# Context projections of a decoder layer's fold as three products of split operands, split by GpSimd

## The chip, the cores and the metric

The kernel runs on 1 core of a Trainium2 chip. The metric is the device time of one execution in microseconds (us). The five engines of the core are named as in the profile: PE (TensorE matmul) and PEld (its weight loads), DVE (VectorE), ACT (ScalarE), POOL (GpSimd) and SP (SyncE, which here only issues DMAs).

## The reference, cut to what matters

One decoder layer on `x` of 4 batches x 1024 rows x 256: a gated recurrence, then a cross attention over 64 context rows per batch plus one "null" row, then a feed-forward layer with weights quantised to three values and activations to 8 bits. The change concerns how keys and values of the cross attention are made, and what follows at once:

```python
q = split_heads(einsum('bnd,df->bnf', x, Wq)) * 64 ** -0.5         # 16 heads of 64
kv = einsum('bmc,cf->bmf', context, Wkv)                           # context 4 x 64 x 512, Wkv 512 x 2048
k, v = split_heads(kv[..., :1024]), split_heads(kv[..., 1024:])    # a null key and a null value are put before them
attn = softmax(einsum('bhid,bhjd->bhij', q, k))
out = merge_heads(einsum('bhij,bhjd->bhid', attn, v))
out = einsum('bnf,fd->bnd', out, Wout)
x = x + layernorm(out) * ln_scale + ln_bias
x = x + bitlinear(silu(gate(z)) * up(z), w_down)                   # z = layernorm(x), the feed-forward layer
```

## The kernel before, in words

Each engine has its instruction stream written out by hand, in the order in which it is executed; semaphores tie the streams together. There is no scheduler: an engine that waits holds back all that is written behind the wait.

**Stage 1** (`stage1`, `groups`) runs over 8 groups of 4 tiles of 128 rows: normalise, transpose, project with fp32r products of split operands (a high and a low part, three products: hi x hi, lo x hi, hi x lo), sigmoid, scan on DVE, residual. At its end lie the ternary quantisation of the feed-forward weights (`rounded` on POOL, L520 and L523; `ternary` on DVE, L903) and, for the last groups, the statistics of the second layernorm (`stats2` on DVE up to L914; POOL raises them to a power, L533).

**The fold** comes between stage 1 and the loop over tiles. Since the context is small, keys are multiplied into Wq and values into Wout once, so that a tile needs only scores = x * M and out = p * VW. The program numbers 16 projections `kv_T(i)`: 0 to 7 for keys (one pair of heads each), 8 to 15 for values. A projection (L1362 to L1370) is four fp32 products of 128x128 weights with 128x256 of the transposed context `ctxT`; it appears in rows as L1279 with operands `region_b,VW` (keys) or `region_b` alone (values), as 8 records. Then:

- ACT copies it to `kvT` (`put_kvT`, L734), with the null row subtracted.
- `fold_keys(i)` (PE, L1383) multiplies it with Wq's transpose; ACT takes the high part `Mhi` out of PSUM (L742), DVE the low part `Mlo` (L1032). The PE stream runs `kv_T(i + 2)`, `fold_keys(i)` for i = 0 to 7; before the last of them come the transposes of tiles 0 and 1 (`pair_T(0, 0)`, L1419), whose copies are `xT2hi` (ACT, L771) and `xT2lo` (DVE, L1048).
- Then PE runs tile 0's scores (twelve 128x512 fp32r products, L1279 with `Mhi`, `Mlo`, `xT2hi`, `xT2lo`), `kv_T(10)`, `fold_values(0)` (L1400), `kv_T(11)`, `kv_T(12)`, `fold_values(1)`, tile 1's scores, `kv_T(13)`, `kv_T(14)`, `fold_values(2)`, `pair_T(1, 1)`, the null values (L1410), `kv_T(15)`, `fold_values(3)`. The results are copied to `VW` by DVE (`put_values_first`, L1042) and ACT (`put_values_second`, L752).
- Softmax of tiles 0 and 1 runs beside it: maximum and subtraction on DVE (L1065, L1069, L1070), exponential on ACT (L826), sum and reciprocal on DVE (L1076, L1081), multiplication with the reciprocal on POOL (`probabilities`, L577). POOL also sums Wout's blocks for the null value (`wsum`, L554, L557).

**The loop over tiles** (`stages2_3`, n = 0 to 31, then a tail) runs scores of tile n+2, transposes of the probabilities of tile n (L1530, L1538), out of tile n (L1550, L1553, L1558), and the feed-forward layer of earlier tiles (gate, up, down). ACT alternates between the tables of Exp and Silu: it loads Silu at L786, in `silu_gate` (L783 to L792), and Exp at L826. In a step ACT runs `norm_out` (L779), the two copies of `pT` (L857, L860), `silu_gate`, `quantise_h` (L803), `norm3` (L810), `norm2` (L756), `exponential`. On POOL a step has `add_output` (L562 to L566), `probabilities`, `cast_h` (L590), `deviation3` (L609 to L613), `deviation4`, `quantise_z`.

## Time and profile before

| | |
|---|---|
| median of 3 runs | 496.48 us (495.41 to 497.45) |
| the profiled execution | 498.77 us |
| its span, first to last instruction | 497.0 us |
| busy in the span | PE 462.5 us (93%), PEld 362.3 (73%), DVE 401.7 (81%), ACT 329.1 (66%), POOL 308.9 (62%) |
| mean granted TensorE clock | 0.987 of full speed |
| chain of waits, by engine | PE 80%, DVE 6%, POOL 3%, DMA 3%, the rest 2% or less each |

Busy shares are sums over the whole span. The chain of waits is followed back from the last instruction, at each step to what released it; an edit gains time only where it shortens this chain, and no further than to the next chain beside it. In the rows a time is in us from the start of the span unless it is marked ns. A row of a timeline can hold several instructions of one kind ("x8"); neighbours on PE overlap in their records, as a product's end is modelled. Stage 1 ends at about 98.8 us, the fold lasts from there to 158.6 us, the tail begins at about 465 us.

### The profile page before, as it was taken

The page shows a single profiled execution, that of the slowest core. Times are in us where ns is not written, and L with a number is a line of the kernel's source. Part 1 is how long each engine was busy: PE and PEld are TensorE (multiplying, and loading weights), DVE is VectorE, ACT ScalarE, POOL GpSimd, SP SyncE. Part 2 cuts the span into 40 slices and gives each one's busy share as a digit, 9 for nine tenths or more (in the row PEclk, how much of TensorE's full clock was granted, in tenths as well). Part 3 has the DMA queues.
Part 4 walks back from the last instruction along what each step waited for, and adds up shares of the span by engine and source line. Part 5 has one row for each costly group of instructions (what it writes and reads, how often), then busy time and mean ns, then how long its engine had stood idle before and what let it go on. Part 6 is the DMA issues. An engine that isn't in the chain of part 4 may idle for free.

```text
span 497.0 us, 7915 instructions
## 1 busy us (share of the span) xinstructions
PE 462.5 (93%) x2504; PEld 362.3 (73%) x2532; DVE 401.7 (81%) x882; ACT 329.1 (66%) x429; POOL 308.9 (62%) x465
## 2 busy tenths in 40 slices
PE   1989999999799999999999999999999999999664
PEld 0768888777577888787878777778778787876332
DVE  4789988974455688999989989899898998995883
ACT  4556543245335354898888888889788888886560
POOL 2234555650011468788788788787877878878850
PEclk9999999999899999999999999999999999999996
DMA  8997000240000000012232121212222222222352
GB/s 263 325 365 272 3 0 1 42 86 0 1 1 1 1 0 7 7 32 45 51 44 49 38 58 39 54 38 47 50 44 48 52 45 44 49 43 53 65 120 65
DMA packets 67129, 31.72 MB, mean 64 GB/s; under 512 B 49680, under 2 KB 65296, under 8 KB 67088
## 3 DMA queue, kind: packets, MB, share of 16 engines
q1 hardware_dynamic: 67088, 31.21, 25.0%
q8 instruction: 21, 0.34, 0.3%
q14 instruction: 20, 0.16, 0.1%
HBM read 15.21 MB, written 4.19 MB: 39 GB/s over the span
## 4 chain that ended last, share of the span: by engine, by line
PE 80%; DVE 6%; POOL 3%; DMA 3%; SPq 2%; issue 2%; ACT 2%; another core or an unknown queue 0%; DVEq 0%; ACTq 0%; POOLq 0%
PE psum L1279 37%; PE psum L1553 10%; PE psum L1558 10%; PE psum L1295 10%; DMA xs<-in_x_dram 3%; PE psum L1530 3%; PE psum L1538 2%; SPq L409 2%; PE psum L1383 2%; PE psum L1419 2%; PE psum L1400 2%; PE psum L1314 1%; PE psum L1330 1%; DVE amax L1112 1%; PE psum L1550 1%
## 5 line engine op out<-in xcount | busy, mean ns | idle before, releaser
L577 POOL TENSOR_TENSOR region_d<-region_d,rden 128x1024 f32<-128x1024 f32 x30 | 57.1, 1905 | 13.4 <-DVE rden L1081 13.1
L1553 PE MATMUL psum<-VW,region_d 128*128 128x256 f32 x256 | 60.6, 380 | 0.2
L1558 PE MATMUL psum<-VW,region_d 128*128 128x256 f32 x256 | 60.5, 379 | 0.0
L1279 PE MATMUL psum<-Mhi,xT2hi 128*128 128x512 f32 x128 | 54.2, 424 | 3.3 <-DVE xT2lo L1048 3.3
L1065 DVE TENSOR_REDUCE mx<-psum 128x8 f32<-128x512 f32 x64 | 44.0, 687 | 15.5 <-PE psum L1279 14.5
L1105 DVE SCALAR_TENSOR_TENSOR region_c<-psum,hzw,region_c 128x1024 f32<-128x1024 f32 x32 | 41.1, 1283 | 17.0 <-ACT region_c L791 16.8
L1558 PEld LDWEIGHTS psum<-VW,region_d 128*128 128x128 f32 x256 | 48.6, 190 | 6.6
L1553 PEld LDWEIGHTS psum<-VW,region_d 128*128 128x128 f32 x256 | 46.3, 190 | 6.5 <-ACT region_d L857 0.6
L1279 PE MATMUL psum<-Mhi,xT2lo 128*128 128x512 f32 x128 | 50.9, 397 | 0.0
L1279 PE MATMUL psum<-Mlo,xT2hi 128*128 128x512 f32 x128 | 50.4, 394 | 0.0
L1070 DVE SCALAR_TENSOR_TENSOR region_d<-mx,psum 128x512 f32<-128x512 f32 x60 | 40.9, 681 | 1.0
L529 POOL TENSOR_TENSOR pw_out<-pw_in,expo 128x8 f32<-128x8 f32 x8 | 13.2, 1648 | 43.1 <-DVE pw_in L943 43.1
L1112 DVE TENSOR_REDUCE amax<-region_c 128x1 f32<-128x1024 f32 x32 | 39.0, 1218 | 0.9
L1279 PE MATMUL psum<-wgT,region_d 128*128 128x512 bf16 x123 | 32.3, 379 | 5.7 <-DMA region_d<-region_c 5.5
L791 ACT ACTIVATE region_c<-psum,hzw 128x1024 f32<-128x1024 f32 x32 | 35.7, 1114 | 2.4 <-remote 1.7
L803 ACT ACTIVATE region_c<-region_c,qr 128x1024 int16<-128x1024 f32 x31 | 35.3, 1139 | 2.3 <-DVE qr L1163 1.9
L1076 DVE TENSOR_REDUCE den<-region_d 128x16 f32<-128x1040 f32 x30 | 36.7, 1223 | 0.0
L826 ACT ACTIVATE region_d<-region_d 128x1040 f32<-128x1040 f32 x30 | 32.2, 1072 | 5.6 <-DVE region_d L1070 5.3
L590 POOL CAST region_d<-region_c 128x1024 bf16<-128x1024 int16 x31 | 32.2, 1038 | 4.5 <-ACT region_c L803 4.5
L1295 PE MATMUL psum<-xT1hi,w1hi 128*128 128x512 f32 x96 | 32.1, 416 | 2.2 <-ACT xT1hi L693 1.2
L786 ACT ACT_TABLE_LOAD x26 | 33.4, 1283 | 0.5
L857 ACT ACTIVATE region_d<-psum 128x512 f32<-128x512 f32 x32 | 19.1, 596 | 21.4 <-PE psum L1530 21.3
(159 smaller groups left out, 1163.5 us busy)
## 6 DMA issues: line engine op xcount, KB each, us to landing
out_dram<-xs SPq DMA_DIRECT2D x32, 128.0 KB, 1.9
xs<-in_x_dram SPq DMA_DIRECT2D x1, 2560.0 KB, 13.7
VW<-in_L_xattn_Wkv_dram SPq DMA_DIRECT2D x1, 2048.0 KB, 12.3
region_b<-in_L_xattn_Wkv_dram SPq DMA_DIRECT2D x1, 2048.0 KB, 16.5
xs<-in_x_dram SPq DMA_DIRECT2D x3, 512.0 KB, 6.5
region_w<-in_L_ffn_w_gate_dram SPq DMA_DIRECT2D x2, 512.0 KB, 9.6
region_w<-in_L_ffn_w_up_dram SPq DMA_DIRECT2D x2, 512.0 KB, 8.0
region_w<-in_L_ffn_w_down_dram SPq DMA_DIRECT2D x8, 128.0 KB, 5.7
```

What stands on the lines that cost most here:

```text
L577: pool.tensor_tensor(p_of(t).rearrange("p (h j) -> p h j", j=MK), e[:, :, 0:MK], rden[:, v, :].unsqueeze(2).broadcast_to([P, H, MK]), ALU. ...
L791: act.activation(hid3[v], banks(gate_bank(n), 2).rearrange("p b n -> p (b n)"), ACT.Silu, scale=hzw[:, (n - 5) % 4, 2:3]).then_inc(silu_re ...
L803: act.activation(nq3, hid3[t % 2], ACT.Copy, scale=qr[:, t % 2, 0:1]).then_inc(hq_done, 1)
L1065: dve.tensor_reduce(mx[:, hh, :], scores, AX.X, ALU.max).then_inc(max_done, 1)
L1070: dve.scalar_tensor_tensor(out=e[:, :, 0:MK], in0=mx[:, hh, :].unsqueeze(2).broadcast_to([P, HB, MK]), scalar=0.0, in1=scores, op0=ALU.max ...
L1076: dve.tensor_reduce(den[:, :], e_of(n).rearrange("p (h j) -> p h j", j=J), AX.X, ALU.add) \
L1105: dve.scalar_tensor_tensor(out=hid3[v], in0=banks(2, 2).rearrange("p b n -> p (b n)"), scalar=hzw[:, (n - 5) % 4, 3:4], in1=hid3[v], op0=A ...
L1112: dve.tensor_reduce(amax[:, v, 0:1], hid3[v], AX.X, ALU.max, apply_absolute_value=True) \
L1279: mm = pe.matmul(dst, lhsT, rhs, start=i == 0, stop=i == len(terms) - 1)
L1295: mm = pe.matmul(bank(b), lhsT, rhs, start=i == 0, stop=i == len(terms) - 1)
L1553: pe.matmul(bank(7, D), pT[:, pair, :], VW[:, batch(n), pair, :], start=False, stop=False)
L1558: mm = pe.matmul(bank(7, D), pT[:, pair, :], VW[:, batch(n), pair, :], start=False, stop=pair == HC - 1)
```

## The change

1. **Projections.** `kv_T(i)` becomes twelve fp32r products of 128x256 in place of four fp32 ones: high weights x high context, high weights x low context, low weights x high context (four column blocks each). The last four wait for the low weights alone (`kvw_ready`), the first eight for the high ones (`kvw_hi`).
2. **Splitting.** The context's high part is ACT's copy as before, now as fp32r; its low part is a new 128x1024 subtraction on DVE, put before `ternary(1)`. The weights are split by POOL, 128x512 per projection: a cast to fp32r, then a subtraction (`split_kvw(i)`). There are two buffers, so split i waits for projection i - 2. Splits 0 to 3 lie at the end of POOL's stage 1, 4 to 9 between the additions of `wsum`, 10 to 13 after them, 14 and 15 between `probabilities(0)` and `probabilities(1)`.
3. **Order around tile 0.** `kv_T(10)` goes ahead of tile 0's scores on PE. ACT's `xT2_pair(0, 0)` and DVE's `xT2_lesser(0, 0)` go ahead of the last pair's copies of `M`.
4. **Room.** The split parts use the memory of stage 1's `xT1hi` and `xT1lo`. The exponentials of tiles 0 and 1 lie in the late pairs of `VW` in place of `region_c`, so both `put_values(2)` now wait for `probabilities(1)` (`p_ready` 2). `probabilities` of tiles 0 and 1 is two 128x512 products each. `p` and `pT` lie elsewhere in `region_d`.
5. **ACT's waits.** The wait for the transposed feed-forward weights moves from before `put_kvT(0)` to `put_keys_hi(0)`.
6. **Last steps.** In step 30 ACT loads Silu's table at the start of the step, in place of after the copies of `pT`; in step 31 `silu_gate` comes first on ACT.

```diff
+        ctxThi = xT1hi_flat[:, 0:CC * BM].rearrange("p (k n) -> p k n", k=CC)
+        kvwhi = xT1hi_flat[:, CC * BM:].rearrange("p (r k n) -> p r k n", r=2, k=CC)
+        kvwlo = xT1lo_flat[:, 0:CC * BM].rearrange("p (r k n) -> p r k n", r=2, k=CC)
+        ctxTlo = xT1lo_flat[:, CC * BM:].rearrange("p (k n) -> p k n", k=CC)
...
+        late_pairs = VW[:, :, HC // 2:, :].rearrange("p b c n -> p b (c n)")
+        wsum = VW[:, B - 1, HC - 1, :]
...
+            def split_kvw(i):
+
+                w = (wk if i < HC else wv)[:, :, (i % HC) * P:(i % HC + 1) * P]
+                pool.wait_ge(wk_loaded if i < HC else wv_loaded, 16)
+                if i == 0:
+                    pool.wait_ge(q_psum, NG)
+                if i > 1:
+                    pool.wait_ge(fT_psum, i - 1)
+                pool.tensor_copy(kvwhi[:, i % 2, :, :], w).then_inc(kvw_hi, 1)
+                pool.wait_ge(kvw_hi, i + 1)
+                pool.tensor_tensor(kvwlo[:, i % 2, :, :], w, kvwhi[:, i % 2, :, :].bitcast(F32), ALU.subtract) \
+                    .then_inc(kvw_ready, 1)
...
             groups(stage1)
+            split_kvw(3)
...
             for pair in range(2, HC):
+                split_kvw(pair + 2)
                 pool.wait_ge(wout_summed, pair - 1)
                 pool.tensor_tensor(wsum, wsum, wout[:, pair, :], ALU.add).then_inc(wout_summed, 1)
+            for i in range(HC + 2, HC + 6):
+                split_kvw(i)
...
             probabilities(0)
+            split_kvw(2 * HC - 2)
+            split_kvw(2 * HC - 1)
+            probabilities(1)
...
+                if q == 2:
+                    act.wait_ge(p_ready, 2)
                 act.wait_ge(fold_psum, HC + q + 1)
...
                 if isinstance(g, int) and g == NG - 1:
+                    dve.wait_ge(ctxT_ready, 1)
+                    dve.tensor_tensor(ctxTlo.rearrange("p k n -> p (k n)"), banks(0, 2).rearrange("p b n -> p (b n)"),
+                                      ctxThi.rearrange("p k n -> p (k n)").bitcast(F32), ALU.subtract) \
+                        .then_inc(ctxT_lo_ready, 1)
                     ternary(1)
...
-                w, pair = (wk if i < HC else wv), i % HC
-                group(bank(i % 2, BM), [(w[:, k, pair * P:(pair + 1) * P], ctxT[:, k, :]) for k in range(CC)]) \
-                    .then_inc(fT_psum, 1)
+                pe.wait_ge(kvw_hi, i + 1)
+                for j, (w, c_) in enumerate(((kvwhi, ctxThi), (kvwhi, ctxTlo), (kvwlo, ctxThi))):
+                    if j == 2:
+                        pe.wait_ge(kvw_ready, i + 1)
+                    for k in range(CC):
+                        mm = pe.matmul(bank(i % 2, BM), w[:, i % 2, k, :], c_[:, k, :], start=j == 0 and k == 0,
+                                       stop=j == 2 and k == CC - 1)
+                mm.then_inc(fT_psum, 1)
...
+            kv_T(HC + 2)
             pe.wait_ge(m_lo, 2 * HC)
             for hh in range(2):
                 scores_half(0, hh, 0, 0, 0)
-            kv_T(HC + 2)
             fold_values(0)
```

Where the instructions stand. PE, from the last key fold to the first value fold, before (L1279 with `region_b` is a projection, L1383 the key fold, L1400 the value fold; the rows left out are the rest of tile 0's twelve products):

```order
L1419 MATMUL psum<-ident,region_d 128x128 x4
L1279 MATMUL psum<-region_b 128x256 x4
L1383 MATMUL psum<-region_b,VW 128x256 x4
L1279 MATMUL psum<-Mhi,xT2hi 128x512
L1279 MATMUL psum<-Mlo,xT2hi 128x512
L1279 MATMUL psum<-Mhi,xT2lo 128x512
...
L1279 MATMUL psum<-region_b 128x256 x4
L1400 MATMUL psum<-region_b 64x256 x16
```

The same place now (L1433 is a projection, L1448 the key fold, L1465 the value fold):

```order
L1484 MATMUL psum<-ident,region_d 128x128 x4
L1433 MATMUL psum<-xT1hi 128x256 x4
L1433 MATMUL psum<-xT1lo,xT1hi 128x256 x4
L1433 MATMUL psum<-xT1hi,xT1lo 128x256 x4
L1448 MATMUL psum<-region_b,VW 128x256 x4
L1433 MATMUL psum<-xT1hi 128x256 x4
L1433 MATMUL psum<-xT1lo,xT1hi 128x256 x4
L1433 MATMUL psum<-xT1hi,xT1lo 128x256 x4
L1340 MATMUL psum<-Mhi,xT2hi 128x512
L1340 MATMUL psum<-Mlo,xT2hi 128x512
...
L1465 MATMUL psum<-region_b 64x256 x16
```

A projection has three rows of four products, and projection 10 stands before the scores instead of behind them.

POOL, from its last rounding to tile 0's probabilities, before:

```order
L523 TENSOR_SCALAR region_w<-region_w 128x2048
L533 TENSOR_TENSOR rstd<-ve,expo 128x4 x2
L551 COPY nvsel<-nulls 128x1 x2
L554 TENSOR_TENSOR region_c<-region_b 128x256
L557 TENSOR_TENSOR region_c<-region_c,region_b 128x256 x6
L577 TENSOR_TENSOR region_c<-region_c,rden 128x1024
```

And now, as far as split 4 and the first addition behind it (L543 and L545 are the cast and the subtraction of a split, L556 the power, L585 the addition to `wsum`):

```order
L543 CAST xT1hi<-VW 128x512
L545 TENSOR_TENSOR xT1lo<-VW,xT1hi 128x512
L556 TENSOR_TENSOR rstd<-ve,expo 128x4
L543 CAST xT1hi<-VW 128x512
L545 TENSOR_TENSOR xT1lo<-VW,xT1hi 128x512
L556 TENSOR_TENSOR rstd<-ve,expo 128x4
L543 CAST xT1hi<-VW 128x512
L545 TENSOR_TENSOR xT1lo<-VW,xT1hi 128x512
L579 COPY nvsel<-nulls 128x1 x2
L581 TENSOR_TENSOR VW<-region_b 128x256
L543 CAST xT1hi<-VW 128x512
L545 TENSOR_TENSOR xT1lo<-VW,xT1hi 128x512
```

Splits 2 and 3 stand behind the two powers, which wait for DVE's statistics, and each later addition has a split before it.

DVE, at the end of the last group's work, now (L1053 is the product that was L1003, L1057 the context's low part, L953 `ternary`, L959 to L964 `stats2`):

```order
L1053 TENSOR_TENSOR region_a<-psum,region_a 128x1024
L1057 TENSOR_TENSOR xT1lo<-psum,xT1hi 128x1024
L953 TENSOR_SCALAR region_w<-region_w 128x2048
L969 SCALAR_TENSOR_TENSOR nmr<-mv,rstd 128x4
L959 BN_STATS st<-xs 128x6 x4
```

Before, the row of L1057 was not there and `ternary(1)` followed the product at once.

## Rows read from the trace of the kernel before

**Rows 1.** The page, busy time, share of the span and instructions of each engine
```profile
PE 462.5 (93%) x2504; PEld 362.3 (73%) x2532; DVE 401.7 (81%) x882; ACT 329.1 (66%) x429; POOL 308.9 (62%) x465
```

**Rows 2.** Chain of waits in the fold: start us, length us, what
```profile
127.44 1.09 PE psum L1383 x8
...
128.55 0.61 ACT Mhi L742
...
129.18 1.29 DVE Mlo L1032 x2
130.47 0.61 DVE xT2lo L1048
...
143.08 1.89 PE psum L1400 x32
...
156.62 1.96 PE psum L1400 x32
...
161.07 1.38 PE psum L1279 x6
162.45 0.12 PE psum L1550
```

**Rows 3.** Timeline of PE, projection 10 behind tile 0's scores
```profile
135.24 2.31 PE L1279 MATMUL psum<-region_b 128*128 128x256 f32 x8
```

**Rows 4.** Busy by stretch, tile 0's scores and after: length, engines, granted clock
```profile
131.20:139.40 8.20, 8.19 (x53) 5.97 (x53) 4.07 (x6) 1.43 (x2) 0.00 (x0) 0.79 0.00 0
```

**Rows 5.** Groups of instructions of POOL: busy us, mean ns, idle before
```profile
L577 POOL TENSOR_TENSOR region_d<-region_d,rden 128x1024 f32<-128x1024 f32 x30 | 57.1, 1905 | 13.4 <-DVE rden L1081 13.1
...
L590 POOL CAST region_d<-region_c 128x1024 bf16<-128x1024 int16 x31 | 32.2, 1038 | 4.5 <-ACT region_c L803 4.5
...
L620 POOL TENSOR_SCALAR region_d<-region_d,qr 128x256 f32<-128x256 f32 x32 | 15.4, 482 | 0.6 <-DVE qr L1147 0.6
...
L538 POOL TENSOR_TENSOR xs<-xs,region_b 128x1024 f32<-128x1024 f32 x5 | 12.0, 2396 | 0.0
...
L557 POOL TENSOR_TENSOR region_c<-region_c,region_b 128x256 f32<-128x256 f32 x6 | 4.4, 726 | 0.5
```

**Rows 6.** Timeline of POOL at the end of stage 1
```profile
92.37 3.03 POOL L520 TENSOR_SCALAR region_w<-region_w,wrecip 128x2048 f32<-128x2048 f32 x1
...
106.14 1.01 POOL L533 TENSOR_TENSOR rstd<-ve,expo 128x4 f32<-128x4 f32 x1 [4.24 <-DVE ve L914]
```

**Rows 7.** Timeline of DVE, end of stage 1 and softmax of tiles 0, 1
```profile
85.97 1.20 DVE L926 TENSOR_TENSOR xT1lo<-psum,xT1hi 128x1024 fp32r<-128x1024 f32 x1
...
92.32 1.22 DVE L903 TENSOR_SCALAR region_w<-region_w 128x2048 bf16<-128x2048 f32 x1
...
97.72 1.22 DVE L903 TENSOR_SCALAR region_w<-region_w 128x2048 bf16<-128x2048 f32 x1
...
105.89 0.17 DVE L914 TENSOR_SCALAR ve<-mv 128x4 f32<-128x4 f32 x1
...
139.60 1.25 DVE L1042 COPY VW<-psum 128x512 f32<-128x512 f32 x2
...
151.91 0.25 DVE L1081 RECIPROCAL rden<-den 128x16 f32<-128x16 f32 x1
```

**Rows 8.** Timeline of ACT, context copy and end of the fold
```profile
97.45 1.03 ACT L707 ACTIVATE region_b<-psum 128x1024 f32<-128x1024 f32 x1 [3.99 <-PE psum L1343]
...
153.33 1.08 ACT L752 ACTIVATE VW<-psum 128x512 f32<-128x512 f32 x2 [1.44 <-PE psum L1400]
154.30 0.60 ACT L771 ACTIVATE xT2hi<-psum 128x512 fp32r<-128x512 f32 x1
156.04 0.47 ACT L734 ACTIVATE region_b<-psum,nulls_neg 128x256 f32<-128x256 f32 x1 [1.14 <-PE psum L1279]
```

**Rows 9.** Last steps: table load on ACT (timeline), busy by stretch (PE, PEld, DVE, ACT, POOL)
```profile
449.79 1.28 ACT L786 ACT_TABLE_LOAD   x1
446.80:465.20 18.40, 16.44 (x88) 11.70 (x87) 12.64 (x35) 11.89 (x16) 16.00 (x30) 1.00 0.25 54
```

More of the change, by code:

```diff
@@ L168, in decoder_layer @@
         f = carve(region_b, [("wq", KD * INNER), ("wout", HC * D), ("ctx", 2 * CTX),
-                             ("wv", CC * INNER), ("ctxT", CC * BM),
+                             ("wv", CC * INNER), ("gap", CC * BM),
                              ("kvT", 4 * BM)])
@@ L257, in decoder_layer @@
         ctxT_ready = sem("ctxT_ready")
+        ctxT_lo_ready = sem("ctxT_lo_ready")
+        kvw_hi = sem("kvw_hi")
+        kvw_ready = sem("kvw_ready")
         wqT_psum = sem("wqT_psum")
@@ L546, in stage1 @@
                     rounded(2)
+                    split_kvw(0)
+                    split_kvw(1)
+                if isinstance(g, int) and g == NG:
+                    split_kvw(2)
             groups(stage1)
+            split_kvw(3)
             pool.wait_ge(nvsel_zero, 1)
@@ L629, in stages2_3 @@
                     add_output(n - 1)
-                if exists(n + 1, T):
+                if n > 0 and exists(n + 1, T):
                     probabilities(n + 1)
@@ L737, in put_keys_hi @@
             def put_keys_hi(i):
+                if i == 0:
+                    act.wait_ge(wT_ready[0], 16)
+                    act.wait_ge(wT_ready[1], 16)
                 act.wait_ge(fold_psum, i + 1)
@@ L816, in _ @@
                 put_kvT(i + 1)
+                if i == HC - 1:
+                    xT2_pair(0, 0)
                 put_keys_hi(i)
@@ L825, in exponential @@
                 act.wait_ge(sim_sub, 2 * t + 2)
-                act.activation(e_of(t), e_of(t), ACT.Exp, scale=-1.0).then_inc(exp_done, 1)
-            xT2_pair(0, 0)
+                e = e_of(t) if t < 2 else e2[:, t % 2, :]
+                act.activation(e, e, ACT.Exp, scale=-1.0).then_inc(exp_done, 1)
             put_kvT(HC + 1)
+            put_kvT(HC + 2)
             exponential(0)
-            put_kvT(HC + 2)
             put_kvT(HC + 3)
@@ L849, in stages2_3 @@
                 even = u4 % 2 == 0 and exists(n, T - 4)
+                if n == T - 2:
+                    act.preload_act_table(ACT.Silu)
+                if n == T - 1:
+                    silu_gate(n, v)
                 if exists(n - 1, T):
@@ L861, in stages2_3 @@
                         .then_inc(pT1_ready, 1)
-                if exists(n - 5, T):
+                if exists(n - 5, T) and n < T - 1:
                     silu_gate(n, v)
@@ L1067, in softmax_half @@
                 if hh == 1:
-                    null = e_of(n).rearrange("p (r h j) -> p r h j", r=2, j=J)[:, :, :, MK]
+                    null = e_of(n).rearrange("p r (h j) -> p r h j", j=J)[:, :, :, MK]
                     dve.tensor_scalar(null, mx[:, :, :], 0.0, None, ALU.max).then_inc(shift_done, 1)
```

62 lines of the change are left out of this document (37 added, 25 removed).

## The prediction

> **What bounds the kernel now.** I read the page first: PE is busy for 93% of the span [rows 1], and the chain of waits lies on PE for 80% of it. So an edit must shorten PE's own work or its waits. I then followed the chain through the fold, then the timelines of all engines there. Three things stand in them.
>
> In the key phase PE never waits: the last key fold ends at 127.44 + 1.09 = 128.53 [rows 2]. The way to tile 0's scores is then serial: ACT's copy, DVE's low part, and DVE's low part of the tile, 0.61 + 1.29 + 0.61 us [rows 2], and PE is idle for 2.7 us until 131.2. Behind that wait the granted clock is 0.79 on average over 131.2 to 139.4 [rows 4], a mixture of both levels: tile 0's scores last from 131.2 to 135.24 [rows 3], 4.0 us, whereas six such products at 2.4 GHz take 1.38 us [rows 2], so twelve take 2.76. After the fold's end at 156.62 + 1.96 = 158.58 [rows 2] the loop over tiles is bound by PE, and what the fold gains or loses should pass to the end unchanged.
>
> **The price of a new projection on PE.** The projection of four fp32 products in the slow stretch shows 2.31 us [rows 3]. For a 128x256 product of fp32r the only row is L1550: the next product starts 0.12 us after it [rows 2], about half of the 0.23 us of 128x512. Twelve in a row make 12 x 0.12 = 1.44 us. The other bound is the 128x512 price, 12 x 0.23 = 2.76. I take 0.12, as it is the same shape and type.
>
> **The price of a split on POOL.** No row has a cast of 512 elements to fp32r. L620 does 256 elements in 0.482 us and L590 1024 in 1.038 [rows 5]; between them 512 take 0.67. The subtraction: L557 (256) takes 0.726 and L538 (1024) 2.396 [rows 5], so 512 take 1.28; L577 does 1024 in 1.905, where one operand is 16 values repeated. I take 1.28, since the subtraction, like L538 and L557, reads two full tensors; with L577's rate it would be 0.95. With a hop after each cast a split is S = 2.0 us. Bounds: 0.52 + 0.95 + a hop, 1.55; and the whole 1024-element rows, 1.04 + 1.91 + a hop, 3.0. A split and the addition behind it (0.73 [rows 5] and a hop, 0.8) make 2.8 us per pair. PE needs 1.44 + 1.09 = 2.5 per pair. **POOL becomes the bound of the key phase.**
>
> **When POOL starts.** The context copy ends at 97.45 + 1.03 = 98.48 [rows 8]. DVE waits for it, subtracts for 1.20 (L926 [rows 7] has the same shape) and starts `ternary(1)` at 99.65 instead of 97.72 [rows 7]. All behind it slips by 1.9 us, so the last group's statistics come at 108.0 instead of 106.06 [rows 7], and POOL's power, which waited for them at 106.14 [rows 6], ends at 109.05. Split 3 is queued behind it. From there: split 3 (2.0), the two copies and the first sum (1.05, of it 0.73 as L557), six splits with five additions between them (12.0 + 4.0): split 9 is done at 128.1. Its last four products (0.48) and the last key fold (1.09) follow: **the key phase ends at F = 129.7, 1.2 us later than before.** All PE work before F, split 0 to 2 included, is earlier than its split.
>
> **From F on.** Now `xT2lo` is made before, so scores start at F + 2.0 (0.61 + 1.29 and hops [rows 2]) = 131.7. Projection 10 fits in that gap (its split ends at 130.95), so PE isn't idle and I expect the clock to stay at 2.4 GHz: 2.76 for the scores. The PE work between the scores and the last value fold is now shorter than the softmax beside it, so new waits set the pace:
> - From a tile's scores to its reciprocal takes, for tile 1, from 143.08 + 1.89 = 144.97 [rows 2] to 151.91 + 0.25 = 152.16 [rows 7], 7.2 us. For tile 0: 138.9.
> - `put_values_first(0)` is queued behind it, 1.25 [rows 7]: 140.1. `fold_values(1)` waits for this (PE alone would be there at 139.3), ends at 142.05 with 1.9 [rows 2].
> - Tile 1's scores start there; its reciprocal is at 149.25.
> - `probabilities(1)`, 1.905 in one piece [rows 5], 2.1 in two: 151.35. Split 15 is done at about 148, before it.
> - ACT is held by the new wait for this: `put_values_second(2)` 1.1, `xT2_pair` 0.5, `put_kvT(15)` 0.5 [rows 8]: 153.55.
> - `fold_values(3)` takes 1.96 [rows 2]: **155.5 instead of 158.58, 3.1 us earlier.**
> From F to this end are 25.8 us, where they were 30.05: a gain of 4.25 after F, of which 1.2 are lost before it.
>
> **The last steps.** In step 30 the table load (at 449.79, 1.28 us [rows 9]) moves ahead of the copies, so silu comes some 0.7 us earlier and the copies of `pT` 0.5 later. But from 446.8 to 465.2 POOL runs 30 instructions, busy for 16.0 of 18.4 us with a hop of under 0.1 us behind each [rows 9], and waits for neither. I take 0 to 0.1 us. Two halves instead of one whole of `probabilities(0)` and the moved buffers cost nothing on the path: PE waits elsewhere.
>
> The sum against the profiled execution: 497.0 - 3.1 of span. That execution took 498.77 us with what lies around it; the median of the runs is 496.48, 2.3 lower. I take the gain off the median: **493.4 us**.
>
> **A rule that speaks against the change.** POOL's L520, 2048 elements, took 3.03 us beside DVE's L903 [rows 6, 7], where twice L590's 1.04 [rows 5] would be 2.1. Splits 1 and 2 lie beside `ternary(1)` and `ternary(2)` and may take 1 us more each; both are done before what follows waits for them (the powers wait for DVE until 102.8 and 108.0), so F doesn't move. The Trainium skill (GPSIMD Engine Reference, Key points) says that GpSimd shares its SBUF interfaces with VectorE and contends with instructions in a 2-port mode or with two SBUF inputs. By that rule the key phase is free of it, since DVE's low parts of M read one operand from PSUM. The pair of rows on L520 agrees with the first half; no row shows the second.
>
> **Rivals.**
> 1. *GpSimd is quicker than taken.* With S = 1.55 F is 7 x 0.45 = 3.2 earlier: 126.5, and the time 490.2. For it: L577's rate. Against: L538 and L557 agree on a slower one. Chance 0.2 for clearly quicker (S below 1.8).
> 2. *GpSimd is slower, and the key phase eats the gain.* It decides from S = 2.0 + 3.1 / 7 = 2.44 us on: F is then 132.8. A cast to fp32r from rows with a stride, or a DVE that shares the memory through the whole phase, could do it; with another 1 us per split, as L520 had [rows 6], S = 3.0, F = 136.7, and the time is 500.4. Against: L557 ran in this very phase beside the same DVE work at 0.726. Chance 0.14 (of it 0.09 slower than before by over 0.5%).
> 3. *fp32r at 256 columns isn't faster in a row than at 512.* Then a projection is 2.76 us on PE and a key pair 3.85; seven of them and a tile pair's transposes behind the first key fold, at 110.9 with three such projections ahead of it, make F about 138, and PE's own work after it (six projections 16.6, two scores 5.5, four folds 7.6, transposes and null 1.0) ends at about 169: 507 us. For it: L1550 stands alone between other shapes, no row has two in a row. Against: 0.12 us sufficed there with a new weight load. Chance 0.05.
> 4. *The gain is partly cancelled*: PE now waits about 1 us before key pair 1, at `fold_values(1)` and at `fold_values(3)`; should the clock fall behind one, the scores' loss of 1.3 us comes back, or the softmax chain is longer than tile 1's was: 495 to 496. Chance 0.13.
>
> **How the numbers follow.** The forecast has 0.48, with 492 to 494.6 as its own range (S from 1.8 to 2.15). 0.5%, 2.5 us, is about what a measurement of this kernel can tell from no change; the forecast lies 0.6 beyond it, so I give faster all of rival 1 and three quarters of the forecast: 0.2 + 0.36 = 0.56. Same: the rest of the forecast 0.12, rival 4, and 0.05 of rival 2: 0.30. Slower: 0.14. The range leaves out the quick end of rival 1, the slow half of rival 2 and rival 3: 490.5 to 498.
>
> **What would show it right or wrong.** Right: in the key phase the new products wait for POOL's subtraction, about 2.8 us per pair, and split 9 is done at about 128; scores of tile 0 take 2.8 us with the clock at 1.00; `fold_values(3)` waits for ACT. The POOL rows of the cast (0.67) and the subtraction (1.28) are the first to read. Wrong: PE without waits in the key phase (rival 1), products 0.23 us apart (rival 3), subtractions of 1.7 us or more (rival 2), or a loop over tiles that doesn't keep its distance from the fold.

## The result, and the profile after

| | before | after |
|---|---|---|
| median | 496.7 us (13 runs, 495.41 to 499.77) | 498.19 us (13 runs, 497.68 to 501.05) |
| ratio, 95% interval | | 1.0034 [1.0017, 1.0050] |
| profiled execution, span, mean granted clock | 498.77 us, 497.0 us, 0.987 | 498.17 us, 496.3 us, 0.992 |

The forecast was 493.4 us and a range of 490.5 to 498.0. The change made the kernel slower by 0.34%, within what I had called "same" and 0.2 us outside the range. Measured once more on another chip (a0_again below) it took 497.12 us, ratio 1.0021: inside the range, but again no gain. The page of after, its part on busy time:

```profile
PE 458.8 (92%) x2568; PEld 363.3 (73%) x2596; DVE 406.2 (82%) x883; ACT 328.7 (66%) x429; POOL 340.6 (69%) x499
```

PE is busy for 3.7 us less than in [rows 1], POOL for 31.7 us more, and the median did not fall. The fold tells why. First POOL at the end of stage 1, where [rows 6] had the last power at 106.14 (timeline: start us, length us, instruction, in brackets the idle time before it and what ended it):

```profile
97.80 1.28 POOL L545 TENSOR_TENSOR xT1lo<-VW,xT1hi 128x512 fp32r<-128x512 f32 x1
99.02 0.61 POOL L543 CAST xT1hi<-VW 128x512 fp32r<-128x512 f32 x1
99.71 2.14 POOL L545 TENSOR_TENSOR xT1lo<-VW,xT1hi 128x512 fp32r<-128x512 f32 x1
103.75 1.01 POOL L556 TENSOR_TENSOR rstd<-ve,expo 128x4 f32<-128x4 f32 x1 [1.90 <-DVE ve L964]
104.72 1.68 POOL L543 CAST xT1hi<-VW 128x512 fp32r<-128x512 f32 x1
106.48 1.29 POOL L545 TENSOR_TENSOR xT1lo<-VW,xT1hi 128x512 fp32r<-128x512 f32 x1
109.67 1.01 POOL L556 TENSOR_TENSOR rstd<-ve,expo 128x4 f32<-128x4 f32 x1 [1.90 <-DVE ve L964]
...
111.32 1.29 POOL L545 TENSOR_TENSOR xT1lo<-VW,xT1hi 128x512 fp32r<-128x512 f32 x1
...
125.85 0.74 POOL L585 TENSOR_TENSOR VW<-VW,region_b 128x256 f32<-128x256 f32 x1
126.52 0.62 POOL L543 CAST xT1hi<-region_b 128x512 fp32r<-128x512 f32 x1
127.22 1.29 POOL L545 TENSOR_TENSOR xT1lo<-region_b,xT1hi 128x512 fp32r<-128x512 f32 x1
128.47 0.73 POOL L585 TENSOR_TENSOR VW<-VW,region_b 128x256 f32<-128x256 f32 x1
```

A split undisturbed is 0.61 + 1.28 with a hop, 1.93 us; a split and its addition come every 128.47 - 125.85 = 2.62 us. Splits 2 and 3 stand behind the powers and wait for DVE. DVE at the same place (compare [rows 7]):

```profile
98.27 1.22 DVE L1057 TENSOR_TENSOR xT1lo<-psum,xT1hi 128x1024 fp32r<-128x1024 f32 x1 [0.71 <-ACT xT1hi L749]
99.41 1.30 DVE L953 TENSOR_SCALAR region_w<-region_w 128x2048 bf16<-128x2048 f32 x1
100.64 1.24 DVE L969 SCALAR_TENSOR_TENSOR nmr<-mv,rstd 128x4 f32<-128x4 f32 x1
...
104.72 1.22 DVE L953 TENSOR_SCALAR VW<-region_w 128x2048 bf16<-128x2048 f32 x1
...
106.98 0.80 DVE L969 SCALAR_TENSOR_TENSOR nmr<-mv,rstd 128x4 f32<-128x4 f32 x1
...
109.42 0.17 DVE L964 TENSOR_SCALAR ve<-mv 128x4 f32<-128x4 f32 x1
```

L969 works on 4 elements in each partition and takes 1.24 and 0.80 us. It ends at 101.88 and 107.78, where POOL's subtractions end: 99.71 + 2.14 = 101.85 and 106.48 + 1.29 = 107.77. The last statistics are ready 3.5 us later than in [rows 7] (109.42 against 105.89). PE, the key phase from the third projection on, and its later waits:

```profile
106.55 0.71 PE L1433 MATMUL psum<-xT1hi 128*128 128x256 f32 x4 [2.14 <-POOL xT1hi L543]
...
111.39 0.71 PE L1433 MATMUL psum<-xT1hi 128*128 128x256 f32 x4 [1.76 <-POOL xT1hi L543]
...
112.67 1.03 PE L1433 MATMUL psum<-xT1hi,xT1lo 128*128 128x256 f32 x4
113.63 2.08 PE L1448 MATMUL psum<-region_b,VW 64*128 64x256 f32 x8
115.64 1.03 PE L1433 MATMUL psum<-xT1hi 128*128 128x256 f32 x4
...
126.70 0.74 PE L1433 MATMUL psum<-xT1hi 128*128 128x256 f32 x4
...
128.32 1.13 PE L1448 MATMUL psum<-region_b,VW 64*128 64x256 f32 x8
...
131.91 1.13 PE L1448 MATMUL psum<-region_b,VW 64*128 64x256 f32 x8
...
135.07 0.50 PE L1340 MATMUL psum<-Mhi,xT2hi 128*128 128x512 f32 x1 [0.39 <-DVE Mlo L1086]
...
143.74 1.96 PE L1465 MATMUL psum<-region_b 64*64 64x256 f32 x32 [0.69 <-ACT region_b L773]
...
157.12 1.96 PE L1465 MATMUL psum<-region_b 64*64 64x256 f32 x32 [0.89 <-ACT region_b L773]
```

Two new waits for POOL's casts, 2.14 and 1.76 us, and behind them the key fold takes 2.08 us where its neighbours take 1.13. The windows (length, then busy time of PE, PEld, DVE, ACT, POOL, then the granted clock):

```profile
112.90:116.30 3.40, 3.40 (x15) 2.35 (x15) 0.00 (x0) 0.55 (x2) 3.32 (x5) 0.50 0.00 0
116.30:133.00 16.70, 16.43 (x124) 13.17 (x123) 8.43 (x13) 10.48 (x23) 15.14 (x19) 1.00 0.00 1
```

The granted clock is 0.50 (1.2 GHz) from 112.9 to 116.3, and 1.00 (2.4 GHz) behind that. From there to the last key fold PE never waits but for 0.27 us at the transposes: it isn't POOL that sets the pace of the rest of the key phase. The last key fold ends at 131.91 + 1.13 = 133.04, 4.5 us after [rows 2]. The chain of waits in this stretch goes over POOL's splits and powers to 112.6 and then stays on PE (start us, length us):

```profile
109.67 1.01 POOL rstd L556
110.68 0.56 POOL xT1hi L543
...
111.32 1.30 POOL xT1lo L545
...
112.67 1.03 PE psum L1433 x4
113.70 2.01 PE psum L1448 x8
115.71 1.91 PE psum L1433 x12
117.62 1.06 PE psum L1448 x8
118.69 1.63 PE psum L1433 x12
```

Behind the last key fold it went as forecast. ACT's new wait for both tiles' probabilities is there (timeline of ACT):

```profile
155.08 1.09 ACT L796 ACTIVATE VW<-psum 128x512 f32<-128x512 f32 x2 [2.99 <-POOL region_d L610]
```

### The profile page after: what moved, and what is told of

Its sections match the earlier page's. It is cut to its first block, busy times and chain, and to the rows that moved or that the text cites. A ratio compares the mean times of both kernels' runs of the same rounds, so it can differ in the third digit from the quotient of the medians.

```text
span 496.3 us, 8095 instructions
## 1 busy us (share of the span) xinstructions
PE 458.8 (92%) x2568; PEld 363.3 (73%) x2596; DVE 406.2 (82%) x883; ACT 328.7 (66%) x429; POOL 340.6 (69%) x499
## 4 chain that ended last, share of the span: by engine, by line
PE 76%; POOL 8%; DVE 8%; issue 3%; ACT 2%; DMA 2%; SPq 0%; POOLq 0%; ACTq 0%; DVEq 0%
PE psum L1340 31%; PE psum L1356 10%; PE psum L1623 10%; PE psum L1618 10%; PE psum L1433 3%; PE psum L1595 3%; PE psum L1603 2%; PE psum L1448 2%; PE psum L1484 2%; PE psum L1391 1%; POOL xT1lo L545 1%; PE psum L1465 1%; DMA gcol<-in_L_attn_gamma_dram 1%; PE psum L1375 1%; DMA region_d<-region_c 1%
```

## The experiments

Twelve runs follow, in three groups; each group ran on a chip of its own, and the kernel before ran there too (median 496.80, 496.72 and 497.72 us). The ratios are not the quotients of the two medians and differ from them by up to 0.2% (b2_reorder: 0.9906 against 493.13 / 496.80 = 0.9926), so differences of 0.1% between rows say little. F is the end of the last key fold on PE, E the start of tile 2's scores, which closes the fold; both from the profiled execution, as is the span. The last column is what lies behind the fold. d3_pad_act has no row, since its whole time line is shifted; it is told of below.

| run | median us (runs) | ratio to before [95%] | first key fold | F | E | E - F | span - E |
|---|---|---|---|---|---|---|---|
| before, as first shown | 496.7 (13) | | 105.81 | 128.51 | 158.51 | 30.0 | 338.5 |
| c1_before_again | 497.00 (10) | 0.9991 [0.9968, 1.0013] | 105.69 | 128.38 | 156.80 | 28.4 | 336.6 |
| b1_new_tail | 497.32 (12) | 1.0008 [0.9986, 1.0029] | 105.61 | 128.30 | 156.73 | 28.4 | 338.6 |
| b2_reorder | 493.13 (6) | 0.9906 [0.9882, 0.9929] | 106.02 | 128.72 | 154.94 | 26.2 | 336.4 |
| b2_again | 495.16 (9) | 0.9946 [0.9922, 0.9969] | 105.72 | 128.41 | 154.62 | 26.2 | 338.1 |
| after | 498.19 (13) | 1.0034 [1.0017, 1.0050] | 108.49 | 133.04 | 159.00 | 26.0 | 337.3 |
| a0_again | 497.12 (12) | 1.0021 [1.0002, 1.0040] | 108.59 | 133.17 | 159.10 | 25.9 | 336.9 |
| a1_old_tail | 496.94 (12) | 0.9991 [0.9973, 1.0009] | 108.56 | 132.88 | 158.85 | 26.0 | 336.0 |
| a2_fill | 497.16 (12) | 1.0005 [0.9990, 1.0020] | 108.72 | 131.90 | 157.81 | 25.9 | 337.7 |
| a3_early_splits | 495.88 (12) | 0.9987 [0.9968, 1.0006] | 107.91 | 130.46 | 156.35 | 25.9 | 337.6 |
| a4_ahead | 494.64 (12) | 0.9950 [0.9925, 0.9974] | 107.36 | 129.48 | 155.45 | 26.0 | 337.0 |
| d1_dve_order | 492.56 (6) | 0.9903 [0.9879, 0.9926] | 106.29 | 127.20 | 153.21 | 26.0 | 336.9 |
| d2_pad_pe | 496.24 (10) | 0.9974 [0.9956, 0.9993] | 110.32 | 132.62 | 158.62 | 26.0 | 336.0 |

### First chip: which part of the change costs

**c1_before_again**: the kernel before, unchanged, as a control.

> The kernel before, unchanged, profiled once more. Its profiled execution of before took 498.77 us where the median of its runs is 496.70, and it had a fall of the granted clock at tile 0's scores (132.66 to 136.07 us). Theory A (the fall is a matter of where the chip's clock happens to look at PE, and most executions have none or one that costs less): this profile shows another set of falls, a span of about 495 us, and tile 0's scores in 2.8 us. Then 1.6 of the 4.25 us that the prediction found behind the last key fold were never there in most executions. Theory B (the idle 2.7 us before the scores always bring it): the fall stands at the same place and the scores take 4.0 us again.

Measured 497.00 us, ratio 0.9991. Its profile corrected my base. The stretch that in [rows 4] had a clock of 0.79 in it:

```profile
131.10:156.80 25.70, 25.09 (x206) 18.72 (x206) 13.41 (x22) 9.16 (x17) 3.80 (x2) 1.00 0.01 2
```

There is no fall of the clock in the fold, though PE had been idle for 2.6 us ahead of it as before. So the fold ends at 156.80 and not at 158.51; b1, whose fold is the same, gives 156.73. Of the three profiled executions with this fold, the one that I had read is the untypical one.

**b2_reorder**: the new order around tile 0 alone, in the kernel before; the projections stay four fp32 products, and nothing is split. **b2_again** is the same kernel on the third chip.

```diff
@@ ACT @@
                 put_kvT(i + 1)
+                if i == HC - 1:
+                    xT2_pair(0, 0)
                 put_keys_hi(i)
@@ DVE @@
             for i in range(HC):
+                if i == HC - 1:
+                    xT2_lesser(0, 0)
                 put_keys_lo(i)
-            xT2_lesser(0, 0)
@@ PE @@
+            kv_T(HC + 2)
             pe.wait_ge(m_lo, 2 * HC)
             for hh in range(2):
                 scores_half(0, hh, 0, 0, 0)
-            kv_T(HC + 2)
```

> The kernel before, with fp32 projections and no splitting, and only the order of the change around tile 0: projection 10 ahead of tile 0's scores, the copies of tiles 0 and 1's transposes ahead of the last pair's copies of M. PE's gap of 2.7 us before the scores takes up projection 10 (1.9 us), and 0.7 us of copies leave the serial way. Theory 1 (this part is good and the splitting is what costs): 2.0 to 2.7 us faster, ratio 0.9945 to 0.996, 494.0 to 494.7 us; up to 4 us where the fall of the clock goes as well. Theory 2 (the softmax of tiles 0 and 1 takes over as the bound): the values phase waits for put_values_first(0), gain under 1 us.

> Before with nothing but the new order around tile 0, projections still fp32 in four products; once more, beside the next version on the same chip. Both theories: ratio 0.990 as before, fold ends at about 154.9.

Measured 0.9906 and 0.9946: clearly faster, alone. In the trace F stays (128.72, 128.41) and the fold ends 1.9 and 2.2 us earlier than in c1. The medians fell by more than that (3.7 and 2.6 us against the kernel before on their chips). For b2_reorder most of the rest is the clock. Each run has its mean granted clock on record: the 29 runs of before on that chip lie between 0.984 and 0.995, the six of b2_reorder between 0.993 and 0.997. Over all 84 runs of before on the three chips, the 10 with a clock of 0.984 or 0.985 took 499.1 to 500.1 us, the 22 with 0.994 or 0.995 took 494.9 to 497.3. The profiled spans of c1 and b2_reorder, both at a high clock (0.994 and 0.993), are 2.1 us apart. What a key pair costs with fp32 products is read here as well (timeline of PE):

```profile
113.06 1.99 PE L1281 MATMUL psum<-region_b,VW 128*128 128x256 f32 x8
114.99 1.13 PE L1385 MATMUL psum<-region_b,VW 64*128 64x256 f32 x8
116.05 1.99 PE L1281 MATMUL psum<-region_b,VW 128*128 128x256 f32 x8
```

116.05 - 113.06 = 2.99 us per pair, against 2.69 with split operands (chain of after: 118.69 + 1.63 - 117.62 = 2.70, and 2.69 for the pairs behind it). The split saves PE 0.30 us per pair, 2.1 over seven. DVE's L920, the same instruction as L969 of after, takes 0.15 us here, where POOL waits:

```profile
99.06 0.15 DVE L920 SCALAR_TENSOR_TENSOR nmr<-mv,rstd 128x4 f32<-128x4 f32 x1
```

**a1_old_tail** is the change with the old last steps, **b1_new_tail** the kernel before with the new ones. The edit of b1 (a1 is its inverse):

```diff
-                if n < T - 1:
+                if n < T - 2:
                     act.preload_act_table(ACT.Silu)
...
+                if n == T - 2:
+                    act.preload_act_table(ACT.Silu)
+                if n == T - 1:
+                    silu_gate(n, v)
...
-                if exists(n - 5, T):
+                if exists(n - 5, T) and n < T - 1:
                     silu_gate(n, v)
```

> The changed kernel with the last steps as they were (Silu's table loaded after the copies of pT in step 30, silu_gate behind them in step 31). Theory 1 (the loss is all in the fold): like the changed kernel, ratio to before 1.003, 498.2 us, within 0.3. Theory 2 (the last steps cost: POOL's work of steps 30 and 31 begins 0.64 us later against the out product of step 28 than before): 0.5 to 1.5 us faster than the changed kernel, ratio to before 1.000 to 1.002.

> The kernel before with only the last steps of the change (the table load of step 30 at the step's start, silu_gate first in step 31). Theory 1 (neutral): ratio 0.9995 to 1.0005, 496.7 us. Theory 2 (costs): ratio 1.001 to 1.003, 497.2 to 498.2 us. A gain of over 0.5 us would speak for the step's purpose and against both.

b1 has 1.0008, c1 0.9991: no difference. a1 has 0.9991, where the change has 1.0034 and 1.0021. So in one kernel the last steps do nothing, and in the other they seem to cost up to 0.4%. That looked like an interaction; the third chip's runs explain part of it.

### Second chip: the start of the key phase

**a0_again** is the change unchanged. **a2_fill** puts 14 products on PE before projection 2 and 12 before projection 3, into the bank that the projection then overwrites, so that PE works where it waited.

```diff
+                for r in range({2: 14, 3: 12}.get(i, 0)):
+                    pe.matmul(bank(i % 2, BM), ctxThi[:, r % CC, 0:P], ctxThi[:, r % CC, :], start=True, stop=True)
                 pe.wait_ge(kvw_hi, i + 1)
```

> The changed kernel, unchanged, on the chip of the three below. Theory 1 (its loss is real and repeats): ratio to before 1.002 to 1.005, 498 to 498.5 us, one or two falls of the granted clock in the key phase (107 to 116 us), the fold's end (first score of tile 2) at 159.0 us, where the two profiles of before without a fall in the fold have 156.8. Theory 2 (the earlier 1.0034 was this much by the other chip): 0.999 to 1.001, as with the old last steps.

> The changed kernel with 14 and 12 products more on PE, into the projection's own PSUM bank, which the projection then overwrites: they fill PE's waits for splits 2 and 3 (2.14 and 1.76 us) and do nothing else. Theory C (the granted clock's fall behind these waits is what makes PE late in the key phase, and PE, at 2.69 us per pair against POOL's 2.61, never catches up): clock 1.00 in the whole fold, last key fold ends at 130.1 us instead of 133.0, fold's end at 156.1 instead of 159.0, 2.5 to 3 us faster than the changed kernel, 495.3 us. Theory P (POOL alone sets the pace, the clock's fall hides behind it): no change, within 0.3 us.

In a0 the clock falls at 112.90 as in after. (In a1 it had fallen at 108.4, for 6.8 us, and F is 132.88.) In a2 it does not fall in the fold, and F is 131.90 in place of 133.17, the fold's end 1.3 us earlier. The ratio is 1.0005 against 1.0021; the intervals overlap, so the time alone would not have shown it. I had expected F at 130.1 and the miss told me more than the hit: PE was now at full clock, with waits for POOL of 0.36, 0.15 and 0.16 us only, and still came 1.8 us later than my sum. From split 3 on, PE's own work sets F, not POOL.

**a3_early_splits** puts splits 2 and 3 ahead of POOL's two powers; **a4_ahead** also the nvsel copies, the first addition and split 4 ahead of the last power.

```diff
                     split_kvw(0)
                     split_kvw(1)
+                    split_kvw(2)
                 if isinstance(g, int) and g == NG:
-                    split_kvw(2)
+                    split_kvw(3)
```

> The changed kernel with split 2 ahead of POOL's power for group 6 and split 3 ahead of that for group 7, so that neither waits behind DVE's statistics, which the context's low part delays by 3 us. PE's waits before key pairs 2 and 3 nearly go. Theory Q (queueing behind the powers is what costs): splits 2 and 3 done at 103.9 and 106.9 us instead of 107.8 and 112.6, split 9 at 126.6 instead of 128.5, last key fold ends at 129.3, fold's end at 155.3, 3.5 us faster than the changed kernel, 494.6 us. If only the clock matters and not the queue: as in the run with filling products, 495.3. If neither: 498.

> As the run before it, and also the two copies, the first sum and split 4 ahead of the power of group 7. POOL is then 5 us ahead, and PE at 2.69 us per pair is the bound of the key phase. Last key fold ends at 127.7, fold's end at 153.7, 5 us faster than the changed kernel, 493.0 us, just ahead of the order alone with fp32 projections (493.1 us, fold's end 154.9). If the values phase has a floor in the softmax of tiles 0 and 1 that starts elsewhere, the fold's end stays at 155 or later.

F falls to 130.46 and 129.48 (129.3 and 127.7 had been expected), the fold's end with it, and the ratio to 0.9987 and 0.9950. The waits for POOL's casts at projections 2 and 3 are gone; in a3 there is one of 1.30 us at projection 4 instead, whose split still stands behind the last power, and in a4 none. What was late next shows (PE of a4; its line numbers are moved by three):

```profile
107.36 1.13 PE L1451 MATMUL psum<-region_b,VW 64*128 64x256 f32 x8 [1.41 <-issue]
...
114.00 1.13 PE L1451 MATMUL psum<-region_b,VW 64*128 64x256 f32 x8 [1.20 <-DVE Mlo L1089]
```

The first key fold waits for `wqT`'s second half, which DVE writes from 106.05 to 107.26 behind the residual sum and `ternary(2)` (the row names no releaser, but the fold starts 0.10 us behind this write); the third waits for `Mlo`, which DVE gives only behind the last statistics. Both are DVE's.

### Third chip: the theory whole, and the last steps

**d1_dve_order** is a4 with the rest put right: DVE writes `wqT`'s second half before the last residual sum, the statistics and the shift of the last group go behind the low parts of M of pairs 1 and 3 (the loop over tiles needs them only for its last four tiles), and POOL makes all additions of `wsum` behind split 11, where it waited for 5 us. ACT's first copy to `Mhi` now waits for `ternary(2)` itself.

```diff
@@ DVE, group NG: the second half of wqT @@
                     stats2(g - 2)
+                if isinstance(g, int) and g == NG:
+
+                    dve.wait_ge(wqT_psum, 2)
+                    dve.tensor_scalar(wqT[:, HC // 2:HC, :].rearrange("p c n -> p (c n)"),
+                                      banks(4, 2).rearrange("p b n -> p (b n)"), DH ** -0.5, None, ALU.mult) \
+                        .then_inc(wqT1_ready, 1)
...
-                    dve.wait_ge(wqT_psum, 2)
-                    dve.tensor_scalar(wqT[:, HC // 2:HC, :].rearrange("p c n -> p (c n)"),
-                                      banks(4, 2).rearrange("p b n -> p (b n)"), DH ** -0.5, None, ALU.mult) \
-                        .then_inc(wqT1_ready, 1)
@@ DVE, key pairs @@
                 put_keys_lo(i)
+                if i == 1:
+                    stats2(NG - 1)
+                if i == 3:
+                    shift2(NG - 1)
@@ POOL @@
                     split_kvw(pair + 2)
-                pool.tensor_tensor(wsum, wsum, wout[:, pair, :], ALU.add).then_inc(wout_summed, 1)
+                if pair == 4:
+                    pool.wait_ge(ve2_done, NG)
+                    pool.tensor_tensor(rstd2[:, (NG - 1) * GT:NG * GT], ve2[:, :], expo[:, 0:GT], ALU.pow) \
+                        .then_inc(rstd2_done, 1)
+            split_kvw(HC + 2)
+            split_kvw(HC + 3)
+            for pair in range(2, HC):
+                pool.tensor_tensor(wsum, wsum, wout[:, pair, :], ALU.add).then_inc(wout_summed, 1)
```

> The change with the splits early as in the run before (splits 2 and 3 ahead of the powers, split 4 and nvsel ahead too), and three more moves: DVE makes wqT's second half before the last residual sum, DVE's last statistics and shift go behind the low parts of M of pairs 1 and 3, POOL's last power goes between splits 6 and 7 and all seven sums of Wout's blocks behind split 11. Theory (the start of the key phase costs the split projections their gain; once it is repaired, PE's own pair of 2.69 us is all that is left): key fold 0 starts at 105.95 in place of 107.36, no key fold waits, the last one ends at 105.95 + 1.09 + 7 x 2.69 + 0.8 (transposes) = 126.7 in place of 129.4, the fold ends 26.0 later at 152.7 in place of 155.45, the span is 492.5 - 2.75 = 489.7, and the median about 491.9, ratio 0.990. Rival (POOL binds: its splits cannot come faster than one per 2.6 us): last key fold not before 129, time as before, 494.6. Rival (something behind the fold gives it back: clock falls, code loads, softmax): fold ends at 152.7, span 491.5 or more.

Measured: F 127.20 (expected 126.7), E 153.21 (152.7), span 490.1 (489.7), median 492.56 (491.9), ratio 0.9903 [0.9879, 0.9926] (0.990). No key fold waits (PE):

```profile
106.29 1.13 PE L1463 MATMUL psum<-region_b,VW 64*128 64x256 f32 x8
...
126.07 1.13 PE L1463 MATMUL psum<-region_b,VW 64*128 64x256 f32 x8
```

and now it is POOL that waits for PE, not the other way about:

```profile
120.01 0.61 POOL L543 CAST xT1hi<-region_b 128x512 fp32r<-128x512 f32 x1 [0.70 <-PE psum L1448]
```

This rules out the recorded rival that splits cannot come faster than one per 2.6 us: without the additions between them they come every 1.9. It is faster than the kernel before by 1.0% and so than the change, and on the same chip its median lies below that of b2_again (495.16); its fold ends 1.4 us earlier than b2_again's. From the first key fold to F it takes 20.91 us where b2_again takes 22.69. The split operands are worth something after all, once their start costs nothing; by the traces that is the 1.4 us, the rest between the two medians can be the clock (0.988 to 0.997 in the runs of d1, 0.984 to 0.994 in those of b2_again).

**d2_pad_pe** and **d3_pad_act** are the change with 128 waits more at the start of PE's or of ACT's stream, all of them long fulfilled; they become 64 instructions and so only move the later code in its stream.

```diff
             pe.wait_ge(consts_set, 4)
+            for r in range(128):
+                pe.wait_ge(consts_set, 4)
```

> The change with 64 more instructions at the start of PE's stream (waits that are long fulfilled, while PE waits for its data anyway). Theory (the transpose by DMA that is issued at 473.98 lands after 3.7 us in place of 2.3 because a load of PE's code falls between its issue and its landing): the load moves some 3 to 5 us earlier, the transpose lands after 2.3 us, PE's gate product waits 1.1 us in place of 2.5, the clock does not fall at 478, span 494.3 to 495 in place of 496.3. Rival (the new last steps or this phase of the loop cause it, whatever the code): as the change, 2.2 to 2.5 us of wait, span 496.

> The change with 64 more such instructions at the start of ACT's stream. Theory (PE's code is what is loaded on the queue q8): that load stays at 475, the transpose takes 3.4 to 3.7 us and the gate product waits 2.2 to 2.5 us, span 496; loads on q14 move. If q8 carries ACT's code: the load moves and the wait is 1.1 us, span 494.5.

```profile
q8 instruction: 1, 0.02, 2.2%
...
region_d<-region_c SPq DMA_TRANSPOSE x1, 3.7
```

```profile
477.70 1.50 PE L1340 MATMUL psum<-wgT,region_d 128*128 128x512 bf16 x4 [2.47 <-DMA region_d<-region_c]
```

The same of d2, where the load of code has moved to 458 and none lies in this stretch:

```profile
region_d<-region_c SPq DMA_TRANSPOSE x1, 2.3
```

```profile
475.94 1.79 PE L1340 MATMUL psum<-wgT,region_d 128*128 128x512 bf16 x4 [1.06 <-DMA region_d<-region_c]
```

In d2 the wait is 1.06 us in place of 2.47 (2.21 in a0), and the span 494.6 in place of 496.3 and 496.0, as expected; of these 1.7 and 1.4 us, 0.4 and 0.5 had been won by the end of the fold. Only the clock falls at 476.1 all the same, which I had expected to go. In d3 the load stays where it is in the program, the transpose issued at 478.13 lands after 3.2 us, and the loads on q8 are therefore not of ACT's code. d3 also went wrong in a way of its own: the new waits stand behind ACT's wait for its data and not beside it, and ACT's first copy starts at 11.70 in place of 7.52. All of stage 1 is 4 us later. Three of its executions took 501.42 to 505.26 us (ratio 1.0118), and a fourth 1654.3 us, for which I have no cause; its time says nothing on the question.

d2 also gives the price of the clock's fall in the key phase a second time. There it falls one wait earlier than in after, and is over before split 3 is ready (113.55):

```profile
107.50:110.80 3.30, 3.30 (x14) 3.08 (x16) 2.99 (x11) 0.00 (x0) 1.41 (x2) 0.50 0.84 159
```

The wait that follows takes up most of it (0.62 us in place of 1.76). From the end of split 3 to F are 19.07 us in d2 and 19.05 in a2, and 20.43, 20.44 and 20.26 in after, a0 and a1, where the clock is at 0.50 behind split 3. So a fall there costs 1.2 to 1.4 us.

## Why the prediction was wrong

**The prices held.** The cast was taken as 0.67 and measured 0.61, the subtraction 1.28 and 1.28, a split 2.0 and 1.93. Twelve products were to take 1.44 us and take 1.63 in the stream of key pairs. Rivals 1, 2 and 3 are out by these rows. That split 9 is done at 128.51, where 128.1 was forecast, is luck in part: split 3 came 1.6 us late, and the six splits and additions behind it took 1.15 us less than I had put down, 2.62 us a pair in place of 2.8.

**After F it is right.** From F to the end of the fold 25.8 us were forecast and 26.0 measured, and 25.9 to 26.0 in all eight runs with split operands, with F anywhere between 127.2 and 133.2. The waits at `fold_values(1)` (0.69) and `fold_values(3)` (0.89, behind ACT's wait for POOL's probabilities) are at the places named. At the first, what I had named ends a moment too soon to be the releaser: DVE's `put_values_first(0)` ends at 142.27 + 1.22 = 143.49, ACT's copy of projection 12 at 143.56. b2 has 26.2 with fp32 projections: the gain here is the order's, and the split adds 0.2 us to it, because what PE saves it then stands idle (0.69, 0.29 and 0.89 us before the last three value folds) while the softmax of tiles 0 and 1 sets the pace.

**F is where it failed: 133.04 in place of 129.7.** The step is the sentence "POOL becomes the bound of the key phase", with "All PE work before F, split 0 to 2 included, is earlier than its split". I never added up PE's own work from a late split on. With my own prices, and 0.86 us for the transposes as in the chain of after, it would have been: split 3 done at 111.05, its last products 0.48, seven folds 7.6, six projections 8.6, the transposes 0.86: 128.7, only 1.0 us ahead of POOL. That reserve had to carry three things:
- Split 3 came at 112.61, 1.6 us later. DVE's slip was put at 1.9 us for the context's low part and is 3.5: 1.7 for that subtraction, the rest two instructions of 128x4 elements that were held by POOL's (1.24 and 0.80 us in place of 0.15). The first half of the rule on GpSimd and VectorE was in the prediction, as a price on POOL's splits alone; I didn't charge it on DVE's side, where it delays what POOL then waits for.
- A key pair on PE is 2.69 us, not 2.5; over six pairs 1.0.
- The two waits, 2.14 and 1.76 us, were followed by a clock of 0.50 for 3.4 us. That lengthened the rows at 112.67, 113.63 and 115.64 by 0.4, 0.9 and 0.3 us. a2 gives 1.3 for it, d2 1.4.

1.6 + 1.0 - 1.0 and 1.6 for the clock make 3.2 of the 3.3 us; with the 1.3 of a2 for the clock, 0.4 us stay open. a3, a4 and d1 took these causes away one after another, and F went to 130.46, 129.48 and 127.20.

**The base was wrong too.** I counted as gain that tile 0's scores would run at full clock: 4.0 against 2.76 us. In c1 and b1 they do so before the change. Against c1 the change moves F by +4.7 and what follows by -2.5: the fold ends 2.2 us later. The medians say +1.5 in the first measurement and +0.4 beside a0, whose ratio stands for 1.0 us. Rival 4 had the mechanism (the clock falls behind a new wait and gives a gain back), with the wait at the wrong place and 1.3 us for its price, which is what it cost; it could not have reached 498 alone. The last column of the table spreads by up to 2.6 us, and the clock is the larger part of that: for one kernel, b2, it is 336.4 where the clock is at 0.50 for the last 1.9 us, and 338.1 where it is so for the last 10.7. In before, whose clock falls at 487.6, eight products at 490.93 take 1.88 us on the chain; in c1, with a fall at 491.0, they take 1.05.

**The last steps** were put at 0 to 0.1 us. By c1 and b1 that is what they are worth. In the change they happened to lie with a load of code upon a transpose that PE waits for, for 1.4 us; d2 has the new last steps and no such meeting, and a ratio of 0.9974 in place of 1.0021. The traces carry the 1.4 us (1.2 in a0); that the rest of the distance between the ratios of a1, d2 and the change is chance or clock is likely and not shown. d1 and a3 have such a meeting too (3.6 and 3.4 us to landing).

**Still open.** Why the edit of ACT's last steps moves PE's code load from 475 (after, a0) to 478 (a1) isn't explained by what PE executes, which is the same. Why the clock falls more often in one set of runs than in another isn't known either. With b2 at 0.9906 on one chip and 0.9946 on another, that spread is as large as most of the effects here; for single parts the traces carry the argument, not the medians. The context's low part on DVE, 1.7 of the 3.5 us by which the statistics slipped, was not moved in any run.

## What to carry to other kernels

When work moves to another engine, add up what each engine still has to do from the last late input to the end of the phase, not only the period of the one that looks slowest: PE with 2.69 us per pair behind a POOL with 2.62 never makes up a late start. New work on a side engine is placed by what stands behind it in that engine's queue: here moving statistics out of the way that are needed some 300 us later, with the splits ahead of them, took 5.8 us off F (133.0 to 127.2; it is 128.4 in the kernel before). And take the base from more than one profiled execution before you count a fall of the clock as something to win: the granted clock of every run shows which kind the profile caught.

## What the runs showed of the hardware

**GpSimd and VectorE hold each other up for whole instructions.** The 128x4 instruction L969 of after ends with POOL's subtraction, 101.88 and 101.85, and again 107.78 and 107.77. POOL's cast at 104.72 starts with DVE's `ternary(2)` and takes 1.68 us, the 1.1 us of the other and its own 0.61. In d1 the last statistics were elsewhere and DVE's `ternary(2)` was the one that was held (timeline of DVE in d1):

```profile
106.50 1.92 DVE L964 TENSOR_SCALAR VW<-region_w 128x2048 bf16<-128x2048 f32 x1
108.34 0.15 DVE L980 SCALAR_TENSOR_TENSOR nmr<-mv,rstd 128x4 f32<-128x4 f32 x1
```

It takes 1.92 where it took 1.22, beside a subtraction of POOL that ends at 107.33. The low parts of M, with one operand in PSUM, keep their 1.29 us beside the splits. The Trainium skill (SBUF — State Buffer, Who interferes with whom) states this as an exclusive lock that is held for the whole instruction by whoever starts first, against a VectorE instruction in a 2-port mode or with two SBUF inputs. These rows agree. So a VectorE instruction of 0.15 us that stands on a path has to be priced with up to the full length of GpSimd's instruction beside it.

**A load of code can delay a transpose by DMA.** From 440 us to the end 7 such transposes (L475) run in after, and five land after 2.3 us; the two that take 3.4 and 3.7 are those with a load on q8 that begins between their issue and their landing. In all fourteen profiles 12 of these transposes from 440 us on land late, after 3.1 to 3.8 us, and every one has such a load (two each in after, a0, a1 and d3, one each in a2, a3, d1 and d2); all others land after 2.3. In d2 a load that began 0.6 us before the issue at 459.39 delayed nothing. The loads are single transfers of 0.02 MB, 21 of them in 0.34 MB on q8. The Trainium skill (Runtime: NRT & Kernel Launch, Terms) gives 16 KiB for a block of such a refill, and 0.34 MB / 21 agrees. They moved when PE's stream got 64 instructions more at its start (d2) and stayed at their place in the program when ACT's did (d3), so a change far ahead of a step can cost or give back 1.4 us in it.

**The clock's falls differ between executions of one kernel.** Before: 0.50 from 132.66 on, behind 2.7 us of idle PE; the same code in c1 stays at 1.00 behind 2.6 us. Over 84 runs of that code the mean granted clock is 0.984 to 0.995 and the time 494.9 to 500.1 us, the long ones with the low clock.

**Fulfilled waits aren't free.** The trace of d3 has 64 instructions more on ACT, 77 ns apart, and ACT's first copy is 4.18 us later (the data it waits for came 1 us earlier than in after). On PE, in d2, they are 106 ns apart, and are over at 9.1 us, before PE's first weight load at 10.4: nothing of it is seen, as PE waits for ACT there. PE's first product is 0.5 us later in d2, and so is ACT's first copy, which waits for its data.
